# Second cross-attention: score products in 32-row tiles, and six units masked by VectorE and squared by GpSimd

## The reference

```python
scores = einsum('bqhd,bshd->bhqs', rq, rk) / sqrt(8)
scores = where(mask, -1e32, scores)
t = relu(scores + nbias[0]); t = t * t
attn = t / (t.sum(-1) + 1e-32)
o = einsum('bhqs,bshd->bqhd', attn, rv)
x = x + o @ Wo.T
```

## Time and profile before

| | |
|---|---|
| median of 3 runs | 425.05 us (424.05 to 425.58) |
| the profiled execution | 423.58 us |
| its span | 421.8 us |
| TensorE busy | 389.5 us, 92% of the span |
| VectorE busy | 329.5 us, 78% |
| ScalarE busy | 261.2 us, 62% |
| GpSimd busy | 229.0 us, 54% |

### The profile page before, as it was taken

How to read it: one execution, slowest core, us unless ns; L and a number is a source line. 1 busy time by engine, 2 the same in 40 slices (tenths; PEclk the granted TensorE clock), 3 DMA queues, 4 the chain that set the end, 5 groups by cost and what they waited for, 6 DMA issues and landing times.

```text
span 421.8 us, 8012 instructions
## 1 busy us (share of the span) xinstructions
PE 389.5 (92%) x3110; PEld 317.9 (75%) x3110; DVE 329.5 (78%) x492; ACT 261.2 (62%) x382; POOL 229.0 (54%) x139
## 2 busy tenths in 40 slices
PE   8987999999998999999898888999599999976996
PEld 6765899999997899999897566864366666654795
DVE  3799888898987888987562656997798988953764
ACT  3576788777778778777661355110189989953343
POOL 0032889999779987886430500870097775600034
PEclk9999999999999999999999999999889999999999
DMA  6948877887998778887498003994610000010000
GB/s 201 270 123 199 195 179 177 193 190 178 214 213 176 173 174 183 194 183 167 127 393 322 0 2 62 213 225 100 257 62 2 3 3 2 3 34 0 2 0 14
DMA packets 20014, 57.04 MB, mean 135 GB/s; under 512 B 6528, under 2 KB 8104, under 8 KB 18312
## 3 DMA queue, kind: packets, MB, share of 16 engines
q1 hardware_dynamic: 19976, 56.53, 53.7%
HBM read 18.63 MB, written 0.13 MB: 44 GB/s over the span
## 4 chain that ended last, share of the span: by engine, by line
PE 67%; DVE 11%; SPq 6%; ACT 5%; DMA 5%; issue 4%; POOL 2%; POOLq 0%; ACTq 0%; DVEq 0%
PE ps L948 7%; PE ps L969 6%; PE ps L670 6%; PE ps L672 5%; PE ps L671 5%; PE ps L648 5%; PE ps L649 5%; PE ps L650 5%; SPq L521 4%; PE ps L1042 4%; PE ps L902 3%; PE ps L911 3%; DVE max L1499 3%; DVE y_sq L1489 2%; DMA wkvo_sb<-in_wkvo 2%
## 5 line engine op out<-in xcount | busy, mean ns | idle before, releaser
L390 POOL TENSOR_TENSOR dT_lo<-z_sq,dT_hi 128x1024 fp32r<-128x1024 f32 x56 | 133.3, 2400 | 31.3 <-ACT dT_hi L1071 31.2
L1136 ACT ACTIVATE y_sq<-ps,nmax 128x1024 f32<-128x1024 f32 x64 | 70.8, 1113 | 40.9 <-DVE nmax L1528 38.6
L1499 DVE TENSOR_REDUCE max<-ps 128x1 f32<-128x1024 f32 x64 | 77.9, 1218 | 20.0 <-PE ps L650 19.9
L670 PE MATMUL ps<-dT_hi,ctx_hi 128*128 128x256 f32 x256 | 74.3, 290 | 2.1 <-POOL dT_lo L390 2.1
L1489 DVE STREAM_TRANSPOSE y_sq<-y_sq 128x1024 f32<-128x1024 f32 x60 | 74.0, 1234 | 0.0
L672 PE MATMUL ps<-dT_hi,ctx_lo 128*128 128x256 f32 x256 | 72.4, 283 | 0.0
L671 PE MATMUL ps<-dT_lo,ctx_hi 128*128 128x256 f32 x256 | 72.3, 283 | 0.0
L1646 DVE SCALAR_TENSOR_TENSOR w_ring<-ps,mask_sb 128x1024 f32<-128x1024 f32 x54 | 63.0, 1219 | 5.5 <-PE ps L948 4.3
L1071 ACT ACTIVATE dT_hi<-z_sq 128x1024 fp32r<-128x1024 f32 x60 | 61.5, 1059 | 2.7 <-PE ps L672 2.5
L1268 ACT ACTIVATE p_ring<-w_ring 128x1024 f32<-128x1024 f32 x54 | 55.9, 1056 | 4.5 <-DVE w_ring L1646 2.6
L648 PE MATMUL ps<-ctxT_hi,qk_hi 128*128 128x512 f32 x128 | 52.5, 410 | 4.0 <-ACT y_sq L1136 3.6
(11 more groups left out here) (212 smaller groups left out, 627.5 us busy)
## 6 DMA issues: line engine op xcount, KB each, us to landing
z_sq<-y_sq SPq DMA_DIRECT2D x240, 128.0 KB, 2.4
w_sb<-in_w SPq DMA_DIRECT2D x2, 2048.0 KB, 14.9
kstack<-k_hi SPq DMA_DIRECT2D x16, 256.0 KB, 5.0
ctx_raw<-in_ctx_nat SPq DMA_DIRECT2D x8, 256.0 KB, 8.2
ctxT_raw<-in_ctx_t SPq DMA_DIRECT2D x1, 2048.0 KB, 7.7
kstack<-k_lo SPq DMA_DIRECT2D x8, 256.0 KB, 5.0
wg_sb<-in_wg SPq DMA_DIRECT2D x1, 1088.0 KB, 4.8
wu_sb<-in_wu SPq DMA_DIRECT2D x1, 1088.0 KB, 7.1
```

Of the source, the lines that this page charges most:

```text
L390: return engine.tensor_tensor(d_ring(dT_lo, m), z_chunk(m), d_ring(dT_hi, m), ALU.subtract)
L670: mm(acc, hi[:, k, :], dT_hi[m % 3][:, cols], start=(k == 0), stop=False)
L1136: nc.scalar.activation(out_t, keys, ACT.Exp, bias=nmax[:, hs % 2:hs % 2 + 1], scale=SCALE0, accum_out=rowsum[:, hs, p:p + 1]).then_inc(exp ...
L1499: return v.tensor_reduce(max2[:, 2 * (hs % 2) + p:2 * (hs % 2) + p + 1], slot(2 * hs + p), AX.XY, ALU.max)
```

## The change

- The score products become 32-row tiles. `kstack` is laid out so that four rows per head dimension (high, rest, high, one) stand next to each other: row `4 i + t`. The DMAs write every fourth partition. The ones are a full-width set of group 3 alone, made early by GpSimd, and copied to the groups 0 to 2 by six more DMAs ahead of the others. A head of a group then has 32 rows of its own, and the block-diagonal `qbd` goes.
- `wkvo1` is loaded in five DMAs, since the columns of the key weights are dealt anew; the query weights are laid out the same way by GpSimd (`wq1_rows`). VectorE makes the queries of batch 0 in three operations, GpSimd those of batch 1 in four, between its first two side units, from a copy that ScalarE makes. Signs and bias per row come from reductions of the identity (`row_kind`, `q_signs`, `nb_rows`).
- A pair of units is now the two halves of the heads for the same 128 keys, and one group of sixteen products makes both. The sixteen wait for the reads of units `m-3` and `m-2`. A combo is now every other unit of a batch.
- `SIDE` becomes 0, 6, 12, 18, 24, 32, 38, 44, 50, 56. Six main units (`POOLED`) are read by VectorE as before, but into buffers of their own; GpSimd squares them in place instead of ScalarE. Their V products stand 5.5 units later, as a side unit's do.

```diff
-        SIDE = tuple(range(0, NU - 6, 6))
+        SIDE = tuple(range(0, 25, 6)) + tuple(range(32, 57, 6))
+        POOLED = (15, 21, 27, 35, 41, 47)
+        RING = [m for m in MAIN if m not in POOLED]
-        WEIGHED = sorted(range(NU), key=lambda m: m + SIDE_LAG + 0.5 if m in SIDE else m)
+        WEIGHED = sorted(range(NU), key=lambda m: m + SIDE_LAG + 0.5 if m in SIDE or m in POOLED else m)
...
-            get(wkvo1[:], "wkvo1", "l1w")
+            get(wkvo1[:, 1:3, :], "wkvo1", "l1w", ins["wkvo1"][:, 1:3, :])
+            for g in range(4):
+                get(wkvo1[:, 0, HR * g:HR * g + HR].rearrange("p (r d) -> p r d", r=4), "wkvo1", "l1w",
+                    ins["wkvo1"][:, 0, :].rearrange("p (r g d) -> p g r d", r=4, g=4)[:, g, :, :])
...
             sp.wait_ge(mo_proj, 1)
+            sp.wait_ge(ones_done, 1)
+            for b in range(B):
+                for g in range(3):
+                    keys = slice(b * CTX, (b + 1) * CTX)
+                    sp.dma_start(kstack[3:P:4, g, keys].bitcast(F32), kstack[3:P:4, 3, keys].bitcast(F32))\
+                        .then_inc(ones_in[b], 16)
...
-                    sp.dma_start(kstack[32 * t:32 * t + 32, g, keys].bitcast(F32),
-                                 part[32 * g:32 * g + 32, keys].bitcast(F32)).then_inc(kstack_in[i], 16)
+                    sp.dma_start(kstack[t:P:4, g, keys].bitcast(F32),
+                                 part[HR * g:HR * g + HR, keys].bitcast(F32)).then_inc(kstack_in[i], 16)
...
-            for g in range(4):
-                last = mm(ps[:, 2 + g // 2 * 2, (g % 2) * T:(g % 2 + 1) * T], wq1[:, g, :], xnT[:],
-                          start=True, stop=True)
-                if g % 2:
-                    last.then_inc(q1_psum, 1)
+            for b in range(B):
+                for g in range(4):
+                    last = mm(ps[:, 2 + 2 * b, g * S:(g + 1) * S], wq1_rows[:, g, :], xnT[:, b * S:(b + 1) * S],
+                              start=True, stop=True)
+                last.then_inc(q1_psum, 1)
...
             def scores1(m):
+                b, k = m // (2 * NBLK), block_of(m)
+                for i in range(2):
+                    if m + i >= 3:
+                        slot_read(m + i - 3)
...
-                for a in range(2):
-                    g = 2 * (c % 2) + a
...
-                    last = mm(ps[:, 2 * (m % 3) + a, :], kstack[:, g, at:at + P],
-                              qbd[:, b, g, :, :].rearrange("p h s -> p (h s)"), start=True, stop=True)
-                last.then_inc(s1_psum, 1)
+                for g in range(4):
+                    if k == 0:
+                        pe.wait_ge(kstack_in[4 * b + g], 48)
+                    for r in range(4):
+                        rows, bank = slice(HR * r, HR * r + HR), 2 * ((m + r // 2) % 3) + r % 2
+                        last = mm(ps[:, bank, g * S:(g + 1) * S], kstack[rows, g, at:at + P], q_rows[rows, b, g, :],
+                                  start=True, stop=True)
+                        if g == 3 and r % 2:
+                            last.then_inc(s1_psum, 1)
...
+                elif m in POOLED:
+                    pe.wait_ge(pooled_done, pooled_nth(m))
+                    p = w_pooled[:, (pooled_nth(m) - 1) % 2, :]
...
             for m in range(0, NU + WEIGH_LAG + 1, 2):
-                for i in range(2):
-                    if m + i < NU:
-                        scores1(m + i)
+                if m < NU:
+                    scores1(m)
...
             for m in range(NU):
-                if m % UNITS == SIDE_LAG and m >= UNITS:
-                    copy_o1(m // UNITS - 1)
+                if m == 2 * NBLK + 4:
+                    copy_o1(0)
+                    copy_o1(1)
...
-                if m in SIDE:
+                if m not in RING:
                     continue
...
-            nc.gpsimd.memset(kstack[96:128, :, :].rearrange("p g n -> p (g n)").bitcast(F32), 1.0).then_inc(ones_done, 1)
+            nc.gpsimd.memset(kstack[:, 3, :].bitcast(F32), 1.0).then_inc(ones_done, 1)
...
-                if n + 3 < B * 4:
-                    spread_q(nc.gpsimd, n + 3).then_inc(qbd_pool, 1)
+                for k in POOLED:
+                    if m < k < m + 6:
+                        pool.wait_ge(w1_done, main_nth(k))
+                        w = w_pooled[:, (pooled_nth(k) - 1) % 2, :]
+                        nc.gpsimd.tensor_tensor(w, w, w, ALU.mult).then_inc(pooled_done, 1)
+                if n == 0:
+                    pool.wait_ge(q1b_read, 1)
+                    nc.gpsimd.tensor_scalar(q_high[:, 1, :, :], q_raw[:], SCALE1, None, ALU.mult).then_inc(q1b_part, 1)
...
+                    nc.gpsimd.tensor_tensor(q_rows[:, 1, :, :], q_raw[:], q_part[:, 1, :, :], ALU.add).then_inc(q_made[1], 1)
...
+            link(v.tensor_scalar(flat(q_high), ps[:, 2, :], SCALE1, None, ALU.mult))
+            link(v.tensor_scalar(flat(q_part), flat(q_high), q_signs[:, 1:2], nb_rows[:], ALU.mult, ALU.add))
+            v.scalar_tensor_tensor(flat(q_rows), ps[:, 2, :], q_signs[:, 0:1], flat(q_part), ALU.mult, ALU.add).then_inc(q_made[0], 1)
...
+                if m in POOLED:
...
+                    w = w_pooled[:, (n - 1) % 2, :]
```

More of the change, by code:

```diff
@@ L127, in build @@
         nb_rows = A.take("nb_rows", (P, 1))
+        q_signs = A.take("q_signs", (P, 2))
+        row_kind = A.take("row_kind", (P, 5))
         bias_rows = A.take("bias_rows", (P, 2 * D))
@@ L226, in build @@
         attn_mT = A.take("attn_mT", (P, T))
+        wq_mla = A.take("wq_mla_sb", (P, 2, 4, P))
+        wk_mla = A.take("wk_mla_sb", (P, 5, P))
         clipped = Arena(nc, probs_at, lat_at).take("clipped", (P, 2, 1024))
@@ L462, in side_nth, with ring_nth, pooled_nth, combo @@
             return SIDE.index(m) + 1
+        def ring_nth(m):
+            return main_nth(m) - sum(k <= m for k in POOLED)
+        def pooled_nth(m):
+            return POOLED.index(m) + 1
         MAIN = [m for m in range(NU) if m not in SIDE]
-        WEIGHED = sorted(range(NU), key=lambda m: m + SIDE_LAG + 0.5 if m in SIDE else m)
+        RING = [m for m in MAIN if m not in POOLED]
+        WEIGHED = sorted(range(NU), key=lambda m: m + SIDE_LAG + 0.5 if m in SIDE or m in POOLED else m)
         def weighed_nth(m):
             return WEIGHED.index(m) + 1
-        def combo_weighed(c):
-            return max(weighed_nth(m) for m in range(c * UNITS, (c + 1) * UNITS))
+        def combo(m):
+            return m // (2 * NBLK) * 2 + m % 2
+        def block_of(m):
+            return m % (2 * NBLK) // 2
+        def of_combo(c):
+            return [weighed_nth(m) for m in range(NU) if combo(m) == c]
         block = ctx.enter_context(nc.Block())
@@ L802, in _ @@
             pe.wait_ge(load["ctxT2"], 16)
-            pe.wait_ge(load["l1w"], 16)
+            pe.wait_ge(load["l1w"], 16 * 5)
             fill(0)
@@ L956, in weigh_v @@
                 b, n = c // 2, weighed_nth(m)
-                first = n == min(weighed_nth(i) for i in range(c * UNITS, (c + 1) * UNITS))
+                first, final = n == min(of_combo(c)), n == max(of_combo(c))
                 if first and c >= 2:
@@ L971, in weigh_v @@
                                   p[:, (2 * j + a) * S:(2 * j + a + 1) * S],
-                                  start=first and a == 0, stop=n == combo_weighed(c) and a == 1)
+                                  start=first and a == 0, stop=final and a == 1)
                 last.then_inc(pv1_done, 1)
@@ L1606, in _ @@
             link(v.tensor_tensor(eq, onehot[:], bc(rtm[:, 0, :], 2, E0), ALU.mult))
+            for i, (first, every) in enumerate(((3, HR), (7, HR), (0, 4), (1, 4), (2, 4))):
+                v.tensor_reduce(row_kind[:, i:i + 1], ident[:, first:P:every], AX.X, ALU.add).then_inc(kinds_done, 1)
             dve.wait_ge(load["mask"], 16)
             for n, m in enumerate(SIDE):
-                at = m // (2 * UNITS) * NBLK + m % UNITS
+                at = m // (2 * NBLK) * NBLK + block_of(m)
                 v.tensor_scalar(cap_side[:, n, :], mask_sb[:, at, :], 0.0, None, ALU.is_equal).then_inc(cap_side_done, 1)
@@ L1639, in _ @@
             for m in MAIN:
-                c, at = m // UNITS, main_nth(m)
                 dve.wait_ge(s1_psum, m + 1)
-                if at > 3:
-                    dve.wait_ge(sq_done, at - 3)
+                if m in POOLED:
+                    n = pooled_nth(m)
+                    if n == 1:
+                        for i in range(B * 4):
+                            dve.wait_ge(kstack_in[i], 48)
+                    if n > 2:
+                        dve.wait_ge(pv1_done, weighed_nth(POOLED[n - 3]))
+                    w = w_pooled[:, (n - 1) % 2, :]
+                else:
+                    n = ring_nth(m)
+                    if n > 3:
+                        dve.wait_ge(sq_done, n - 3)
+                    w = w_ring[:, (n - 1) % 3, :]
```

136 lines of the change are left out of this document (64 added, 72 removed).

## The result

The changed kernel takes 436.69 us, the median of 5 runs (435.70 to 441.18); the kernel before took 425.58 beside it (424.05 to 427.87). The ratio is 1.0273, with an interval of 1.0230 to 1.0317: slower, as forecast (433.2, range 426.5 to 441), by 3.5 us more than forecast. The profiled execution is the longest of the five, 441.18 us with a span of 439.2; the other four have spans of 433.3 to 435.1. Its mean granted clock is 0.946, theirs 0.956 to 0.964.

The account below looks back on a forecast made before the run. TensorE was taken to bound the kernel in the second cross-attention. Stage +6.9, queries -0.2 and load +1.5 make +8.2 us: 431.8 from the profiled 423.58, 433.2 from the median 425.05; range 426.5 to 441.

Parts of the forecast that it names:

- The chain behind V product 17: Scores 20 and 21 queue behind it; its square waits behind unit 18's ReLU: 3.4 us from group (18,19) to (20,21).
- the long stretches: Units 18 to 24, 24 to 30, 38 to 44, 44 to 50, 50 to 56: 7.7 us each instead of 6.37.
- 30 to 56: From unit 30's score group to unit 56's: 32.1 us instead of 28.43, +3.7.
- The score group: Sixteen products in four row tiles on TensorE take 0.70 us instead of 1.12; range 0.48 to 1.13.
- Rival 2: Rounded f32 loses its pace at 128 columns: score group stays 1.12 us, about +6 more, 439.5 us; chance 0.12.
- The stretch 12 to 18 comes out as long: Also 7.7 us: GpSimd makes batch 1's queries, unit 6's square is late, unit 12's ReLU waits for its buffer.
- The load, +1.5: wkvo in five loads, K's weights in 32-byte pieces, on the path ahead of the stage: +1.5 us, range 0 to 4.8.
- add nothing of their own: The MLA weights queue behind the wkvo load and come later by the same, with no extra cost.
- The clock: Full clock assumed in the stage; a rival had a quarter of it at 1.2 GHz, +6 us, 439; chance 0.10.
- The tail, "-0.4": From unit 56's score group to the end of the stage's last copy: 11.6 us instead of 12.03.
- 0 to 12, "12.4": From unit 0's score group to unit 12's: 12.4 us instead of 12.82, group 2 no longer waiting behind VectorE's queries.
- Rival 1: VectorE becomes the bound, 417.9 us; needs group (20,21) within some 1.3 us of group (18,19); chance 0.11.

Follow-up runs that it names:

- e3: Changed kernel plus four products of zeros ahead of each V product but a combo's first, to hold the clock; 433.49 us, 1.0169 of the kernel before.
- e1: Changed kernel with the V products one unit later in TensorE's order (WEIGH_LAG 4 instead of 3); 428.15 us, 1.0062 of the kernel before.
- e8: e1 plus zero products ahead of each V product and ahead of the stage and its first three score groups; 427.62 us, 1.0040 of the kernel before.
- e11: e1 with each pair's sixteen score products issued unit by unit, each unit waiting for its own read; 425.21 us, 0.9968 of the kernel before.
- e5: Changed kernel with the edits of e1 and e3 together; 426.93 us, 1.0015 of the kernel before.
- e9: e8 with GpSimd making batch 1's queries behind side unit 6 instead of side unit 0; 431.55 us, 1.0135 of the kernel before.

## Why the prediction was right or wrong

- **The sign and the mechanism** were right. The chain behind V product 17 is there step by step, the long stretches are 7.75 us where the clock holds (7.7), and 30 to 56 is 32.3 us in e3 (32.1). Undoing it in two ways took back 8.5 and 6.1 us.
- **The score group** was 0.70; it is 0.67, with 0.60 to the next product. The Trainium skill (TensorE: Matmul & The Clock Gate, "Measured speedup vs the span model") gave 0.55, as an estimate by its factor for products of 512 columns; the trace lies between. The 0.70 was put together from the price of V products, another kind of product, so that it came within 0.03 is in part luck. Rival 2 falls with this line.
- **"The stretch 12 to 18 comes out as long"** was a term of its own, and is no fixed size: 6.40 us in e3, 7.69 in the profiled execution, 8.59 once the start is fast. The reason was right (the ReLU of 12 waits for GpSimd); its size hangs on how early unit 12 comes.
- **The load, +1.5**, was wrong: the traces show nothing of it. The Trainium skill (DMA: Bandwidth & Descriptors, "Measured (HBM→SBUF, 128 partitions, SWDGE, issued from GpSimd)") made it 1.3, as an estimate; no run here shows that either. Both priced the pieces one after another behind the load's old landing; the last piece lands no later than the one load did. Why, whether it is the backlog of other loads, is not shown. That the MLA weights "add nothing of their own" was not quite right: their second load is issued at 229.64 us in e1, 224.66 before, and in e1 the chain that ended last runs over it, with the MLA scores 0.4 us later behind the start of the K products than before. In the profiled execution of the changed kernel they are later by the K products' half clock alone.
- **The clock** was the step that failed. The forecast took the full level throughout and gave a rival with a lower one 0.10 and 6 us. It fell in the stage of the changed kernel behind its waits. Beside the stall, holding it from 313 us on is worth 3.2 us by e3. That this is nearly the 3.5 us by which the forecast was low is luck: without the load (1.5) and with 12 to 18 as in e3 (1.3 less) the same sum gives about 430.4, and 6 us are missing. The rest can lie where e3 too has half clock: its units 0 to 12 take 15.36 us where 12.4 were forecast, and the part behind the last copy 47.6 us, 46.2 before. **The tail, "-0.4"**, held to the last copy and was not followed farther: behind it the profiled execution is 2.9 us longer, nearly all of it TensorE's zero products at 1.2 GHz (3.56 and 5.56 us instead of 2.76 and 3.62). **0 to 12, "12.4"**, is right at full clock (e8) and 13.78 here.
- **Rival 1** needed the group within 1.3 us; in e1 it is 2.30 us, with the wait for the square gone, and even e11, whose reads follow each other without a gap for six units, gives 425.2 and not 417.9: the start, the queries' stretch and the clock behind the stage remain.

Open: why the clock fell at the K products in three of the traces (the 4.51 us at 231.36 above, e5 and e9) and not in the others; and what decides on the clock behind the stage, where TensorE has the same idle times of 1.13, 0.93 and 1.56 us in the traces in which it falls (e1, e8) and in those in which it doesn't (e5, the kernel before). A version of e11 with the queries spread over two side units was not tried.

## What to carry to other kernels

Shortening work on the engine that sets the pace pays only if the next wait in its order isn't a longer one; here one number in that order was worth 8.5 us. When a busy TensorE becomes one with gaps, price its lower clock, in the stage and behind it, as part of the change. Work that is put in to hold the clock belongs on the list too: where it stands on the path, it takes longer at the lower clock.

## What was not expected of the hardware

Each time the granted clock fell inside the stage, TensorE had sat idle for over 1 us shortly before: 1.22 us up to 321.57 ahead of the 0.50 from 324 us in the changed kernel, and between 1.03 and 3.4 us in the other traces. With no idle time over 0.64 us (e1, 315 to 345) it stayed at 1.00, with TensorE busy 23.37 of 30.00 us. It stayed in e3 with idle times of 1.00 us, after one of 1.22 us in the changed kernel itself (up to 373.47), and after one of 2.15 us in e8, so not every gap is followed by a fall. These are rows beside each other; only e3 against the changed kernel is an experiment on it.

Row tiles work on by themselves: a product follows the one ahead of it in its own tile by 0.11 us (the changed kernel's group at 370.62), and units issued one behind the other in different tiles overlap (0.69 us for sixteen, 0.66 for eight, e11).
